# The last fifteen groups of an attention kernel and the output projection put into one block of engine programs

## What is computed

```python
x = layernorm(x + self_attention(x))              # 16 batches of 112 tokens, D = 256
q, k, v = x @ Wq, ctx @ Wk, ctx @ Wv              # 8 heads of 128; 1792 queries, 6000 keys
sim = (q @ k.T) * 128 ** -0.5
sim = (sim - sim.mean(-1)) * 1.5 + sim.mean(-1)   # the mean drops out of the softmax
o = softmax(sim) @ v                              # all queries against all keys, in each head
x = layernorm(x + o @ Wout + bout)
h = gelu(x @ ternary(W1).T + b1)                  # 256 -> 1024
x = layernorm(x + h @ ternary(W2).T + b2)         # 1024 -> 256
```

## Time and profile before

| | |
|---|---|
| median of three runs | 2355.7 us (2354.69 to 2356.75) |
| profiled execution, its own time | 2358.36 us |
| its span, first to last instruction | 2356.6 us |
| TensorE busy | 2281.6 us, 97% |
| VectorE, ScalarE, GpSimd busy | 86%, 79%, 79% |
| granted TensorE clock, mean | 0.993 |
| A657 begins | 2205.85 us |
| A671 ends | 2235.3 us |
| T5 begins | 2256.94 us |

### The profile page before, as it was taken

How to read it: one execution, slowest core, us unless ns; L and a number is a source line. 1 busy time by engine, 2 the same in 40 slices (tenths; PEclk the granted TensorE clock), 3 DMA queues, 4 the chain that set the end, 5 groups by cost and what they waited for, 6 DMA issues and landing times. The chain is left out here.

```text
span 2356.6 us, 67328 instructions
## 1 busy us (share of the span) xinstructions
PE 2281.6 (97%) x28774; PEld 2033.9 (86%) x28774; DVE 2016.9 (86%) x2210; ACT 1873.0 (79%) x2227; POOL 1866.2 (79%) x1124
## 2 busy tenths in 40 slices
PE   7988999999999999999999999999999999999797
PEld 3547998899989998899888998999889998999785
DVE  7878888888888888888887888888888888888766
ACT  4347888888888888888887888888888888888844
POOL 8743888798888888888877897888888887899612
PEclk9999999999999999999999999999999999999999
DMA  7401000000000000000000000000000000010220
GB/s 204 149 19 33 4 7 13 4 6 4 13 6 4 6 13 4 6 4 7 13 4 7 4 13 4 7 6 4 13 7 4 7 4 6 7 42 7 84 81 32
DMA packets 34843, 50.79 MB, mean 22 GB/s; under 512 B 2304, under 2 KB 27376, under 8 KB 34544
## 3 DMA queue, kind: packets, MB, share of 16 engines
q1 hardware_dynamic: 34544, 46.45, 6.2%
HBM read 30.97 MB, written 15.47 MB: 20 GB/s over the span
## 5 line engine op out<-in xcount | busy, mean ns | idle before, releaser
L1156 POOL TENSOR_TENSOR e_lo<-ring,e_hi 128x1024 f16<-128x1024 f32 (+1 forms) x665 | 1386.8, 2101 | 200.8 <-ACT ring L660 173.1
L801 DVE TENSOR_TENSOR run_max<-psum,run_max 128x1024 f16<-128x1024 f32 (+1 forms) x616 | 738.5, 1199 | 205.0 <-ACT ring L643 204.0
L643 ACT ACTIVATE ring<-psum 128x1024 f32<-128x1024 f32 (+1 forms) x672 | 673.8, 1003 | 186.1 <-PE psum L346 127.1
L822 DVE SCALAR_TENSOR_TENSOR ring<-ring,psum 128x1024 f32<-128x1024 f32 (+1 forms) x672 | 793.1, 1187 | 0.7 <-PE psum L578 0.7
L346 PE MATMUL psum<-qx_hi,k_hi 128*128 128x256 f16 x2632 | 718.6, 273 | 14.7 <-DVE qx_lo L789 5.9
L370 PE MATMUL psum<-v_main,e_hi 128*128 128x129 f16 x4032 | 718.7, 220 | 6.5 <-POOL e_lo L1156 6.3
L346 PE MATMUL psum<-qx_hi,k_lo 128*128 128x256 f16 x2632 | 718.2, 273 | 2.2 <-issue 2.2
L372 PE MATMUL psum<-v_main,e_hi 128*128 128x128 f16 x4032 | 719.2, 222 | 0.0
L346 PE MATMUL psum<-qx_lo,k_hi 128*128 128x256 f16 x2632 | 718.3, 273 | 0.0
L374 PE MATMUL psum<-v_main,e_lo 128*128 128x129 f16 x4032 | 717.2, 219 | 0.0
L660 ACT ACTIVATE ring<-ring 128x1024 f32<-128x1024 f32 (+1 forms) x672 | 696.2, 1036 | 1.6 <-ACT e_hi L650 0.4
(11 more groups left out here) (195 smaller groups left out, 2793.4 us busy)
## 6 DMA issues: line engine op xcount, KB each, us to landing
o_scratch<-o_buf SPq DMA_DIRECT2D x56, 128.0 KB, 1.9
raw<-o_scratch SPq DMA_DIRECT2D x14, 512.0 KB, 3.6
stage<-in_ctxT SPq DMA_DIRECT2D x6, 500.0 KB, 4.1
stage<-in_ctxT SPq DMA_DIRECT2D x12, 250.0 KB, 5.0
w_scratch<-wall SPq DMA_DIRECT2D x1, 2304.0 KB, 10.5
wall<-w_scratch SPq DMA_DIRECT2D x6, 384.0 KB, 3.3
x<-in_xT SPq DMA_DIRECT2D x4, 448.0 KB, 6.2
res<-in_x SPq DMA_DIRECT2D x1, 1792.0 KB, 14.8
```

Source lines behind the costliest of these rows:

```text
L643: a.activation(ring[:, f % SLOTS, 0:n], pair(f)[:, 0:n], ACT.Copy).then_inc(s_kept, 1)
L801: ins = v.tensor_tensor(run_max[:, 0:n], pair(f)[:, 0:n], run_max[:, 0:n], ALU.max)
L822: v.scalar_tensor_tensor(slot, slot, LIFT, psum[:, 6, 0:QB].unsqueeze(1).broadcast_to([P, t, QB]), ALU.add, ALU.subtract).then_inc(s_sub, 1)
L1156: g.tensor_tensor(e_lo[f % NEL][:, 0:n], slot, e_hi[f % NEH][:, 0:n], ALU.subtract).then_inc(s_lo, 1)
```

## The change

The two blocks become one. The transposes of tiles 0 to 4 and the projections of tiles 0 to 3 are issued between the weighted values of the last fifteen groups: T0 follows A657, T1 follows A660, and so on every third group; P0 is cut into three pieces (3, 3 and 2 of the 8 heads) that follow A660, A661 and A662, P1 into three after A663 to A665, and so on to P3 after A669 to A671. ScalarE's and VectorE's halves of `oT` are put between their work on the groups. Then come T5, P4, T6 and all the rest in the order that it had. In the last fourteen groups GpSimd makes `e_hi` of the odd groups again, as in the groups before them, and VectorE makes their `e_lo` from it; ScalarE no longer makes the second exponential there. Buffers of the later stage move off memory that the attention still uses, P2 and P3 (tiles 2 and 3) use bank 3, P4 and P5 bank 2, and SyncE loads the tiles inside the first block.

```diff
-               for r, o in enumerate((VREG, VREG + 4096, WREG, KREG + 14336, KREG + 18432))]
+               for r, o in enumerate((VREG, VREG + 4096, WREG, RING, RING + 4096))]
...
+        TAIL = NF_ALL - 15
+        O_TURN = {3 * i: i for i in range(5)}
+        O_PROJECT = {3 * i + 3 + x: (i, range(*w)) for i in range(4) for x, w in enumerate(((0, 3), (3, 6), (6, 8)))}
...
+        def bank_of_projection(p):
+            return (7, 3, 2)[p] if p < 3 else 6
...
+                def o_transposes(i):
+                    pe.wait_ge(s_raw[i % NRAW], 16 * (i // NRAW + 1))
+                    if i:
+                        pe.wait_ge(t_lo, i)
+                    else:
+
+                        pe.wait_ge(s_max, NF_ALL)
...
+                def o_project(i, heads=range(NH)):
+                    p = i // 2
+                    if heads[0] == 0:
+                        pe.wait_ge(t_lo, i + 1)
+                        if i == 0:
+
+                            pe.wait_ge(s_free, len(SIDES))
+                            pe.wait_ge(s_late, 48)
+                        elif i == 6:
+
+                            pe.wait_ge(s_sub, NF_ALL)
...
+                    turn = n * NGRP + s - TAIL
+                    if turn in O_PROJECT:
+                        o_project(*O_PROJECT[turn])
+                    if turn in O_TURN:
+                        o_transposes(O_TURN[turn])
...
                     a.wait_ge(s_sub, f + 1)
-                    if f >= LATE:
-                        a.wait_ge(s_hi, f - LATE // 2 + 1)
-                    elif f % 2 == 0:
+                    if f % 2 == 0:
                         a.wait_ge(s_hi, f // 2 + 1)
...
+                def o_high(i):
+                    a.wait_ge(t_tr, i + 1)
+                    if i >= 2:
+                        a.wait_ge(t_wp, i - 1)
...
                     weights = f + EXP_AHEAD
-                    if (weights % 2 == 0 or weights >= LATE) and 0 <= weights < NF_ALL:
+                    if weights % 2 == 0 and 0 <= weights < NF_ALL:
                         exp_half(weights)
...
+                    if f - TAIL in O_TURN:
+                        o_high(O_TURN[f - TAIL])
...
                 def low_weights(f):
                     n = cols_of(f % NGRP)
-                    v.wait_ge(s_exp, f + 1)
+                    v.wait_ge(s_cast, f // 2 + 1)
...
+                    if f - TAIL - 1 in O_TURN:
+                        o_low(O_TURN[f - TAIL - 1])
+                v.wait_ge(s_back, 16)
+                first_residual(0)
                 invert_sums(NBLK - 1)
+                first_residual(1)
+                second_statistics(0)
+                o_low(5)
...
-                    if f >= LATE and f % 2:
-                        continue
                     g.wait_ge(s_exp, f + 1)
...
                         g.tensor_copy(e_hi[f % NEH][:, 0:n], slot).then_inc(s_cast, 1)
+                        if f >= LATE:
+                            continue
                         g.wait_ge(s_cast, casts)
...
                     sp.wait_ge(s_od, (NBLK - NQB + i // QT + 1) * 16)
-                    sp.dma_start(raw[i][:, :, :].rearrange("p h d -> p (h d)"),
-                                 o_part[i * P:(i + 1) * P, :]).then_inc(s_raw[i], 16)
+                    if i >= NRAW:
+                        sp.wait_ge(t_tr, i - NRAW + 1)
+                    sp.dma_start(raw[i % NRAW][:, :, :].rearrange("p h d -> p (h d)"),
+                                 o_part[i * P:(i + 1) * P, :]).then_inc(s_raw[i % NRAW], 16)
...
-                        for i in range(3, NRAW):
+                    if n == NBLK - 3:
+
+                        sp.wait_ge(s_lo, LATE)
+                        for i in range(3, 6):
                             load_tile(i)
...
+                    if n == NBLK - 2:
+                        for i in range(6, 10):
+                            load_tile(i)
+                for i in range(10, NTL):
+                    load_tile(i)
```

More of the change, by code:

```diff
@@ L581, in spread @@
                     mm.then_inc(s_bc, 1)
+                def o_transposes(i):
[4 more added lines that the diff above has]
+                        pe.wait_ge(s_max, NF_ALL)
+                    for h in range(NH):
+                        mm = pe.transpose(psum[:, h // 4, (h % 4) * P:(h % 4 + 1) * P], raw[i % NRAW][:, h, :],
+                                          ident[:, :])
+                    mm.then_inc(t_tr, 1)
@@ new lines, in n_transposes @@
+                def n_transposes(p):
+                    pe.wait_ge(t_n, 2 * p + 2)
+                    if p:
+                        pe.wait_ge(t_yl, p)
+                    else:
+                        pe.wait_ge(s_oev, NBLK * QT)
+                    for r in range(2):
+                        for k in range(2):
+                            mm = pe.transpose(psum[:, 5, k * 2 * P + r * P:k * 2 * P + (r + 1) * P],
+                                              norm2[(2 * p + r) % 4][:, k * P:(k + 1) * P], ident[:, :])
+                    mm.then_inc(t_nt, 1)
@@ new lines, in up @@
+                def up(c, turns):
+                    pe.wait_ge(t_yl, pairs_before(c + 1))
+                    n_cols = columns(c)
+                    for f in turns:
+                        turn = c * NF + f
+                        if turn >= 3:
+                            pe.wait_ge(t_ge, turn - 2)
+                        for n, (k, y) in enumerate([(k, y) for k in range(2) for y in (yT_hi, yT_lo)]):
+                            mm = pe.matmul(psum[:, 2 + turn % 3, 0:n_cols], lhsT=w1t[:, k, f * P:(f + 1) * P],
+                                           rhs=y[:, k, FIRST[c] * P:FIRST[c] * P + n_cols],
+                                           start=(n == 0), stop=(n == 3))
+                        mm.then_inc(t_f1, 1)
@@ new lines, in down @@
+                def down(p):
+                    c = chunk_of(2 * p)
+                    if p == 0:
+                        pe.wait_ge(t_add, 3)
+                    elif p == 5:
+                        pe.wait_ge(t_add, 7)
+                    else:
+                        pe.wait_ge(t_add2, 5 if p == 6 else p)
+                    for r in range(2):
+                        cols = slice((2 * p + r - FIRST[c]) * P, (2 * p + r - FIRST[c] + 1) * P)
+                        for n, (f, y) in enumerate([(f, y) for f in range(NF) for y in (hT_hi, hT_lo)]):
+                            if r == 0 and y is hT_hi:
+                                pe.wait_ge(t_hl, c * NF + f + 1)
+                            mm = pe.matmul(psum[:, bank_of_output(p), r * D:(r + 1) * D],
+                                           lhsT=y[c % 2][:, f, cols], rhs=w2t[:, f, :],
+                                           start=(n == 0), stop=(n == 2 * NF - 1))
+                    mm.then_inc(t_f2, 1)
@@ L629, in _ @@
                 blocks((NH - 2) * NQB, NBLK)
+                o_transposes(5)
+                o_project(4)
+                o_transposes(6)
+                n_transposes(0)
+                o_project(5)
+                o_transposes(7)
+                n_transposes(1)
+                o_project(6)
+                for c in range(2):
+                    i = 4 * c + 8
+                    up(c, range(0, 4))
+                    o_transposes(i)
+                    o_project(i - 1)
+                    up(c, range(4, 8))
+                    o_transposes(i + 1)
+                    o_project(i)
+                    down(2 * c)
+                    if c == 0:
+                        o_transposes(i + 2)
+                    n_transposes(2 * c + 2)
+                    o_project(i + 1)
+                    down(2 * c + 1)
+                    n_transposes(2 * c + 3)
+                    if c == 0:
+                        o_transposes(i + 3)
+                        o_project(i + 2)
+                up(2, range(0, 4))
+                n_transposes(6)
+                up(2, range(4, 8))
+                up(3, range(0, 8))
+                for p in range(4, 7):
+                    down(p)
             @block.scalar
@@ L1070, in _, with keep @@
+                second_norms(3)
+                third_norms(1)
+                hidden_low(2, range(0, 4))
+                n_low(6)
+                hidden_low(2, range(4, 8))
+                hidden_low(3, range(0, 8))
+                second_residual(4)
+                second_residual(5)
+                third_statistics(2)
+                second_residual(6)
+                third_norms(2)
+                third_statistics(3)
+                third_norms(3)
             @block.gpsimd
             def _(g):
+                def keep(c):
+                    for i in tiles(c):
+                        g.wait_ge(t_n, i + 1)
+                        g.tensor_tensor(res2[:, i, :], norm2[i % 4][:, :], b2_b[:, :], ALU.add).then_inc(t_cp, 1)
@@ L1072, in _, with cast @@
+                def cast(c, turns):
+                    n_cols = columns(c)
+                    for f in turns:
```

(23 more changed lines are left out.)

513 lines of the change are left out of this document (201 added, 312 removed).

## The result

The changed kernel took 2341.07 us (median of four runs, 2339.18 to 2342.15) against 2355.87 for the kernel before: a ratio of 0.9935, 95% interval 0.9923 to 0.9946. The forecast was 2341.4.

The account below looks back on a forecast made before the run. ScalarE was taken to bound the last groups, TensorE after the change. Work and borders put T5 at 2241.22, plus 1.45 stall 2242.67, 14.3 us earlier: 2355.7 - 14.3 = 2341.4 us, range 2339.5 to 2344.

Parts of the forecast that it names:

- All is decided by when T5 begins.: Last stretch: order after T5 is unchanged and takes 99.66 us, so each microsecond T5 comes earlier comes off the end.
- TensorE's work without a break, 34.97 us.: From 2205.85 to T5: 13 full groups 17.81, 2 short 2.06, 5 transposes 4.50, 4 projections 10.60 us.
- The 0.40 for cutting P into pieces: Before T5: eight more borders between kinds of TensorE work, at 0.05 us each, add 0.40 us.
- The stalls at the start, 1.45 us.: First interleaved groups: TensorE waits 0.35 us before A659 and 1.1 us before A660, as nothing has run ahead.
- every second group waited about 1.3 us: Last groups before the change: every second group begins after about 1.3 us of waiting on GpSimd's `e_lo`.
- The ports wait for each other.: Before A660: VectorE and GpSimd share an SBUF read port as an exclusive lock, making the stall 1.1 us, not 0.4.
- The removed exponential was the bound, and removing it is what lets T and P fit.: Last groups: without it ScalarE needs 5.8 us per three groups, under TensorE's 7.76, so TensorE becomes the bound.
- my split of the gain: Before T5: 9.6 us won in the last groups, 6.5 in the stretch behind them, less 0.40 and 1.45.
- Rival 1: Last groups: blocked port makes VectorE the bound, losing about 5.5 us; gain 8.8, 2346.9 us; chance 0.15.
- VectorE's `e_lo` at times far over 1.23 us: Profile sign named for the forecast being right: VectorE's `e_lo` sometimes lasts far longer than 1.23 us.
- Rivals 2 to 4: To the end: no waits, 2338.2 to 2339.7 us (0.08); interleaving fails, 2353.4 (0.03); clock at 1.2 GHz, 2376 (0.02).
- rival 2: Nothing waits at all, or the last stretch shrinks too: gain 16 to 17.5, 2338.2 to 2339.7 us; chance 0.08.

Follow-up runs that it names:

- the run with the PSUM operand: Changed kernel, but VectorE's subtraction for odd groups of the last fourteen takes its second input from PSUM, not SBUF (weights not right): 2340.55 us, executed once.
- the second cast: Changed kernel, but GpSimd casts each odd group of the last fourteen again, into memory nobody reads: 2341.22 us, 0.9936 of the kernel before.
- the second subtraction: Changed kernel, but GpSimd does an extra subtraction for each odd group of the last fourteen, into memory nobody reads: 2348.64 us, 0.9966 of the kernel before.

## Why the prediction was right, and where it was not

- *All is decided by when T5 begins.* Right: 99.61 us behind it, 99.66 before, and the same waits.
- *TensorE's work without a break, 34.97 us.* Right within 0.2. The prediction counts a stall from the instant at which TensorE could have gone on; by that count the waits were 0.22 before A659 and 1.05 before A660 (the profile's 0.88 begins 0.16 later, at the modelled end of the last matmul), so the work is 36.08 - 1.27 = 34.81 us. The 0.40 for cutting P into pieces was nothing.
- *The stalls at the start, 1.45 us.* They were 1.27: 0.22 instead of 0.35, and 1.05 instead of 1.1. That the second came out so close is partly luck, as VectorE held GpSimd for 0.39 us and not for 0.7, while without the port the stall is 0.64 (the run with the PSUM operand, by the same count) and not 0.4. The three terms (0.16 in the work, 0.40 for the pieces, 0.18 in the stalls) are what T5 came earlier than forecast: 15.0 us gained instead of 14.3. The median fell by 14.8. The prediction also says that every second group waited about 1.3 us before the change and names 2211.41 for it; the row there has 0.88, and nothing in the sum rests on it.
- *The ports wait for each other.* Right, and shown by the PSUM operand. What it costs TensorE is 0.39 us for the whole stretch. The Trainium skill ("SBUF — State Buffer", Who interferes with whom) says that the one that comes second is blocked to the end of the first; the 2.52 and 3.08 us agree with it to 0.13 us, and so does 2.13 without a second SBUF input.
- *"The removed exponential was the bound, and removing it is what lets T and P fit."* This step failed, and it was luck that the sum didn't suffer: only the two stalls in it belong to the new division, and those are 0.39 us longer than with the old one. Interleaving alone has the full gain. I worked out ScalarE's load for the new division (5.8 us for three groups) and never for the old: 3 x 2.09 + 1.02 = 7.3, which is under 7.76 too. ScalarE was the bound only as long as TensorE had 1.37 us of work for a group of 2.09; as soon as T and P lay between, it wasn't. And where they don't lie between, the new division is no faster, as its ring of waits takes 4.24 us for a pair. For the same reason my split of the gain (9.6 us from the gaps, 6.5 behind them) says only where the room was, not which edit used it: 2.35 came from the border, 13.05 from interleaving, and -0.39 from the division.
- *Rival 1, VectorE blocked.* It had the wrong victim, and so had the sign "VectorE's `e_lo` at times far over 1.23 us": in the changed kernel none is over 1.23, and three of GpSimd's subtractions are 2.49 to 3.08 instead of 2.13. VectorE's subtraction is released by the very cast that ends on GpSimd. Wherever the two meet in the changed kernel it has started first (by 0.14 us before the 3.08), and GpSimd waits. Where VectorE does come second, it pays: with the old division its last `e_lo` starts while GpSimd is still busy, and takes 1.31 instead of 0.95. The cover is wide: GpSimd's 2.1 us more for a pair (the second cast, held by VectorE) cost 0.4 us in the steady part, and 6.31 us for a pair break it.
- *Rivals 2 to 4.* There were two stalls, and the last stretch did not shrink, so rival 2 did not come. From A661 to T5 TensorE did not wait at all, and the clock was 1.00 in that stretch. ScalarE's longest waits there (2.60 and 3.77 us) were for TensorE's transposes, as the prediction has it.

## What to carry to other kernels

Work that is serial for its latencies (a transposition, two halves, a projection) belongs between the last steps of the stage ahead of it, where TensorE has gaps: here its waits vanished there, and so did the fall of the clock behind them (1.00 from A657 to T5). That holds as long as no long wait is left: behind one of 2.48 us the clock fell again. Before an engine is relieved, add up its load for the order that will be there, not for the one that is: here the bound that the second edit removes had already been covered by the first. And an edit of several parts should be tried as a square; one of the parts may do nearly all (here 13.05 of 15.01 us).

## What was not expected of the hardware

With one core's three engines handing a pair around, no engine over 84% busy (GpSimd, 24.90 of 29.83 us), the time for a pair was 4.24 us, set by a ring of waits and in-order queues that no view of busy time shows. And of two engines that become ready through the same semaphore event, VectorE started 0.05 us ahead of GpSimd itself (2219.13 against 2219.18, with the second subtraction; 2210.75 against 2210.78 with the second cast), so that it had the shared port first, each time.
